# Three products of rounded operands for the routed experts' down product

## What is computed

```python
h = jnp.einsum('nd,edh->enh', xf, We1) + be1[:, None, :]
act = _geglu(h)                       # a * gelu(g), 2*768 -> 768
yE = jnp.einsum('enh,ehd->end', act, We2) + be2[:, None, :]
yr = jnp.einsum('end,ne->nd', yE, w)  # two of 12 experts for each token
return (ys + yr).reshape(B, T, Dm)    # ys: a shared expert, 512 wide
```

## Time and profile before

| | |
|---|---|
| median of 3 runs | 1599.58 us (1596.09 to 1599.82) |
| the profiled execution | 1594.34 us |
| its span, first to last instruction | 1592.6 us |
| mean granted clock of TensorE | 0.975 of full speed |
| PE busy | 1355.6 us (85% of the span) |
| DVE, ACT, POOL busy | 1341.0, 1052.6, 999.5 us |
| first routed tile starts | 1329.31 us into the span |
| start of one steady routed tile to the next | 8.51 us |

### The profile page before, as it was taken

How to read it: one execution, slowest core, us unless ns; L and a number is a source line. 1 busy time by engine, 2 the same in 40 slices (tenths; PEclk the granted TensorE clock), 3 DMA queues, 4 the chain that set the end, 5 groups by cost and what they waited for, 6 DMA issues and landing times. The chain is left out here.

```text
span 1592.6 us, 33551 instructions
## 1 busy us (share of the span) xinstructions
PE 1355.6 (85%) x12668; PEld 1021.4 (64%) x12668; DVE 1341.0 (84%) x1691; ACT 1052.6 (66%) x2450; POOL 999.5 (63%) x832
## 2 busy tenths in 40 slices
PE   5899999999999999878676766776766899999992
PEld 4688888888888888765333333333333688888881
DVE  4799999999999999986599999999999635666662
ACT  4666666666666666535599899899899235555550
POOL 1878888888888888647466666667666341332323
PEclk9999999999999999998899999999999999999996
DMA  4511111111111111006651210200000026888872
GB/s 128 183 43 37 49 37 43 36 50 36 43 43 43 43 36 29 2 1 145 146 114 37 22 25 1 42 5 1 1 2 1 1 71 271 301 307 312 307 259 86
DMA packets 104156, 132.87 MB, mean 83 GB/s; under 512 B 39515, under 2 KB 95266, under 8 KB 100553
## 3 DMA queue, kind: packets, MB, share of 16 engines
q1 hardware_dynamic: 91496, 59.85, 15.1%
q0 software_dynamic: 9312, 67.90, 12.0%
q10 hardware_dynamic: 3200, 3.15, 0.6%
HBM read 110.44 MB, written 14.45 MB: 78 GB/s over the span
## 5 line engine op out<-in xcount | busy, mean ns | idle before, releaser
L555 POOL TENSOR_TENSOR half<-prob 128x512 f32<-128x512 f32 (+1 forms) x208 | 266.9, 1283 | 108.0 <-ACT prob L591 106.5
L587 ACT ACTIVATE prob<-ps_s,mx 128x64 f32<-128x64 f32 (+1 forms) x624 | 152.1, 323 | 235.8 <-DVE prob L700 235.8
L1345 DVE TENSOR_TENSOR state<-ps_u,state 128x1024 f32<-128x1024 f32 x252 | 296.7, 1219 | 4.3
L695 DVE TENSOR_REDUCE mx<-ps_s 128x16 f32<-128x1024 f32 (+1 forms) x208 | 253.1, 1217 | 15.9 <-PE ps_s L628 12.0
L1304 PE MATMUL ps_y<-state,cz 128*32 128x256 f32 x2048 | 247.0, 383 | 2.1 <-DVE state L1345 1.1
L628 PE MATMUL ps_s<-qbd,kT 64*128 64x256 f32 (+1 forms) x1664 | 216.8, 395 | 23.3 <-ACT prob L587 17.7
L1231 ACT ACTIVATE ps_a<-A,dt 128x256 f32<-128x256 f32 x504 | 210.4, 463 | 39.5 <-DVE state L1340 39.5
L700 DVE TENSOR_TENSOR prob<-ps_s,mx 128x832 f32<-128x832 f32 (+1 forms) x208 | 213.0, 1024 | 7.1
L1215 POOL TENSOR_TENSOR state<-direct,state 128x1024 f32<-128x1024 f32 x64 | 151.7, 2370 | 88.6 <-PE ps_y L1304 88.6
L1286 PE MATMUL ps_u<-x_rows,b_diag 48*128 48x256 bf16 x1024 | 79.0, 274 | 147.6 <-DVE state L1345 134.9
L628 PEld LDWEIGHTS ps_s<-qbd,kT 64*128 64x128 f32 (+1 forms) x1664 | 150.5, 184 | 67.6 <-issue 35.1
(11 more groups left out here) (257 smaller groups left out, 3116.7 us busy)
## 6 DMA issues: line engine op xcount, KB each, us to landing
raw<-in_ctxT_dram SPq DMA_DIRECT2D x80, 268.0 KB, 2.8
x_rows<-ssm_x SPq DMA_DIRECT2D x96, 64.0 KB
raw<-in_ctxT_dram SPq DMA_DIRECT2D x16, 261.0 KB, 2.8
b_diag<-zeros SPq DMA_DIRECT2D x2, 2048.0 KB, 9.0
x_slots<-zeros SPq DMA_DIRECT2D x1, 3456.0 KB, 14.1
xg<-x_slots SPq DMA_DIRECT2D x27, 128.0 KB, 5.9
y_slots<-y SPq DMA_DIRECT2D x27, 128.0 KB, 4.8
ssm_x<-xp ACTq DMA_DIRECT2D x8, 384.0 KB, 4.8
```

The costliest lines, as they stand in the source:

```text
L555: pool.tensor_tensor(half[0:rows, :, :], prob[0:rows, g % SLOTS, :, 0:L // 2], prob[0:rows, g % SLOTS, :, L // 2:L], ALU.add).then_inc(hal ...
L695: nc.vector.tensor_reduce(mx[0:rows, g % 2, :], part, AX_X, ALU.max, negate=True)\
L1345: nc.vector.tensor_tensor(h, flat(ps_u[k % 2][:, :, :]), h, ALU.add).then_inc(state_ready, 1)
```

## The change

The down product of the routed experts is done as the up products are: w2 (whole, 128 x 1536) and the turned hidden tile are split into high and low parts in F32R, and PE sums high x high, low x high, high x low. For it:

- ACT makes w2's high part (`split_down_high`) once a tile, right behind the gelu of half 0. It writes the hidden tile's high part where it wrote the F32 copy.
- POOL makes w2's low part (`split_down`) once a tile. In its program the subtraction for tile i-2 stands between the load of w1 and the load of w2 for tile i; the two last ones follow behind all loads.
- DVE makes the hidden tile's low part (`take_turned_low`) twice a tile: for the tile before's half 1 behind x low, ahead of w1 low; for this tile's half 0 behind the product for half 1.
- PE waits for w2's low part (w2_split) instead of w2's load.
- Room is made: gel and hid lie in a buffer of the state space block, the gathered rows in w1's buffers.
- The 8 semaphores of the gathers become 4, one for two row blocks. Another semaphore, in the output product of the state space block, is merged with its neighbour.

```diff
@@ start of experts(): buffers
-        w2 = [sbuf(f"w2_{b}", [P, HR // P * D]) for b in range(BUFS)]
+        w2 = [sbuf(f"w2_{b}", [P, HR // P, D]) for b in range(BUFS)]
+        w2l = [sbuf(f"w2l_{b}", [P, HR // P, D], F32R) for b in range(BUFS)]
+        w2h = [sbuf(f"w2h_{b}", [P, HR // P, D], F32R) for b in range(BUFS)]
...
+        gel, hid = (f["spare"][:, i * HR:(i + 1) * HR].rearrange("p (a n) -> p a n", a=2) for i in range(2))
+        hidT = sbuf("hidT", [P, 2, HS // 2])
+        hidTh = sbuf("hidTh", [P, 2, HR // 2], F32R)
+        hidTl = sbuf("hidTl", [P, 2, HR // 2], F32R)
+        back = [w1[t // 6][:, 2 * D * (t % 6):2 * D * (t % 6 + 1)].rearrange("p (i d) -> p i d", i=2) for t in range(TT)]
...
@@ POOL
+            def load_weights(i, m, w, used):
+                if i >= BUFS:
+                    pool.wait_ge(used, 2 * (TT + i - BUFS + 1))
+                pool.indirect_dma_start(w, None, d[("we1", "we2")[m]][:, :],
+                                        bass.IndirectOffsetOnAxis(ap=weight_row[:, i:i + 1], axis=0))\
+                    .then_inc(w_loaded[m][i % BUFS], 16)
+
+            def split_down(i):
+                pool.wait_ge(w2_high, i + 1)
+                if i >= BUFS:
+                    pool.wait_ge(down_done, 2 * (TT + i - BUFS + 1))
+                pool.tensor_tensor(w2l[i % BUFS][:, :, :], w2[i % BUFS][:, :, :], w2h[i % BUFS][:, :, :].bitcast(F32), ALU.subtract)\
+                    .then_inc(w2_split, 1)
+
             for i in range(RTILES):
...
+                load_weights(i, 0, w1[i % BUFS][:, :], values_done)
+                if i >= 2:
+                    split_down(i - 2)
+                load_weights(i, 1, w2[i % BUFS][:, :, :].rearrange("p c n -> p (c n)"), down_done)
+            for i in range(RTILES - 2, RTILES):
+                split_down(i)
...
-                        .then_inc(y_back[t], 16)
+                        .then_inc(y_back[t // 2], 16)
@@ PE, down
+                    passes = [(hidTh, w2h[b]), (hidTl, w2h[b]), (hidTh, w2l[b])]
...
-                        pe.wait_ge(w_loaded[1][b], (turn + 1) * 16)
+                        pe.wait_ge(w2_split, T - TT + 1)
...
                 for c in range(chunks):
...
+                    for i, (rows, weights) in enumerate(passes):
+                        ins = nc.tensor.matmul(ps_y[:, 0:D], rows[:, half, c * P:(c + 1) * P],
+                                               weights[:, half * chunks + c, :], start=False,
+                                               stop=(half == 1 and c == chunks - 1 and i == len(passes) - 1))
@@ ACT
+                    nc.scalar.copy(hidTh[:, half, 0:w], ps_h[half][:, 0:w]).then_inc(hidT_high, 1)
+
+            def split_down_high(T, turn, b):
+
+                act.wait_ge(w_loaded[1][b], (turn + 1) * 16)
+                if not known(turn, 1):
+                    act.wait_ge(down_done, 2 * (T - BUFS) + 2)
+                nc.scalar.copy(w2h[b][:, :, :], w2[b][:, :, :]).then_inc(w2_high, 1)
...
                     gelu(kind, T, turn, b, half)
+                    if kind == "routed" and half == 0:
+                        split_down_high(T, turn, b)
@@ DVE
+            def take_turned_low(kind, T, turn, b, half):
+
+                if kind == "shared":
+                    return
+                dve.wait_ge(hidT_high, (T - TT) * 2 + half + 1)
+                dve.wait_ge(down_done, T * 2 + half - 1)
+                nc.vector.tensor_tensor(hidTl[:, half, :], ps_h[half][:, 0:HR // 2], hidTh[:, half, :].bitcast(F32),
+                                        ALU.subtract).then_inc(hidT_ready, 1)
...
                 if after:
                     take_x_low(*after)
+                if not known(T, 1):
+                    take_turned_low(*behind(kind, T, turn, b, 0, 1))
+                if after:
                     split_low(*after, 0)
                 multiply(kind, T, turn, b, 1)
+                take_turned_low(*behind(kind, T, turn, b, 1, 1))
                 if not known(T, 1):
                     take_y(*behind(kind, T, turn, b, 0, 1)[:4])
...
             def tail():
+                take_turned_low("routed", TT + RTILES - 1, RTILES // BUFS - 1, BUFS - 1, 1)
                 take_y("routed", TT + RTILES - 1, RTILES // BUFS - 1, BUFS - 1)
                 for t in range(TT):
-                    dve.wait_ge(y_back[t], 32)
+                    dve.wait_ge(y_back[t // 2], 64)
```

More of the change, by code:

```diff
@@ L1383, in ssm_output @@
         mean_ready, rr_ready = sem("so_mean_ready"), sem("so_rr_ready")
-        own_ready, rr_placed, rr_taken = sem("so_own_ready"), sem("so_rr_placed"), sem("so_rr_taken")
+        own_ready, rr_placed = sem("so_own_ready"), sem("so_rr_placed")
         shift_chain = sem("so_shift_chain")
@@ L1457, in turn_tokens @@
                 if p == 3:
-                    pe.wait_ge(rr_taken, 1)
+                    pe.wait_ge(rr_placed, 2)
                 for e in range(2):
@@ L1503, in _ @@
             dve.wait_ge(rr_placed, 1)
-            nc.vector.tensor_copy(rr_tokens[:, :], ps_t[3][:, 0, 0:TT]).then_inc(rr_taken, 1)
-            dve.wait_ge(rr_taken, 1)
+            nc.vector.tensor_copy(rr_tokens[:, :], ps_t[3][:, 0, 0:TT]).then_inc(rr_placed, 1)
+            dve.wait_ge(rr_placed, 2)
             for p in range(TT // 2):
@@ L1677, in experts @@
         y_stored = [sem(f"e_y_stored{b}") for b in range(BUFS)]
-        y_back = [sem(f"e_y_back{t}") for t in range(TT)]
+        y_back = [sem(f"e_y_back{p}") for p in range(TT // 2)]
         x_turned, xTh_ready, xT_ready = sem("e_x_turned"), sem("e_xTh_ready"), sem("e_xT_ready")
@@ L1682, in experts @@
         hid_done, hid_turned, hidT_ready = sem("e_hid_done"), sem("e_hid_turned"), sem("e_hidT_ready")
+        hidT_high, w2_high, w2_split = sem("e_hidT_high"), sem("e_w2_high"), sem("e_w2_split")
         down_done, y_taken, out_ready = sem("e_down_done"), sem("e_y_taken"), sem("e_out_ready")
@@ L1766, in _ @@
             pool.wait_ge(owner_ready, 1)
-            for i in range(RTILES):
[L1770 to L1775, removed]
+            def load_weights(i, m, w, used):
[10 more added lines that the diff above has]
+                    .then_inc(w2_split, 1)
+            for i in range(RTILES):
+                load_weights(i, 0, w1[i % BUFS][:, :], values_done)
[4 more added lines that the diff above has]
+                split_down(i)
             for b in range(BUFS):
@@ L1780, in _ @@
                     j = 2 * t + i
-                    pool.indirect_dma_start(back[:, t, i, :], None, d["y_slots"][:, :],
+                    pool.indirect_dma_start(back[t][:, i, :], None, d["y_slots"][:, :],
                                             bass.IndirectOffsetOnAxis(ap=slot[:, j:j + 1], axis=0))\
-                        .then_inc(y_back[t], 16)
+                        .then_inc(y_back[t // 2], 16)
         @block.tensor
@@ L1825, in down @@
                 if kind == "shared":
-                    weights, biases = f["ws2"][:, :, :], f["sel_shared"][:, :]
+                    passes, biases = [(hidT, f["ws2"])], f["sel_shared"][:, :]
                 else:
-                    weights = w2[b][:, :].rearrange("p (c n) -> p c n", c=HR // P)
+                    passes = [(hidTh, w2h[b]), (hidTl, w2h[b]), (hidTh, w2l[b])]
                     biases = sel[:, bass.ds(T - TT, 1), :].rearrange("p a s -> p (a s)")
@@ L1837, in down @@
                 for c in range(chunks):
-                    ins = nc.tensor.matmul(ps_y[:, 0:D], hidT[:, half, c * P:(c + 1) * P],
-                                           weights[:, half * chunks + c, :], start=False,
-                                           stop=(half == 1 and c == chunks - 1))
+                    for i, (rows, weights) in enumerate(passes):
+                        ins = nc.tensor.matmul(ps_y[:, 0:D], rows[:, half, c * P:(c + 1) * P],
+                                               weights[:, half * chunks + c, :], start=False,
+                                               stop=(half == 1 and c == chunks - 1 and i == len(passes) - 1))
                 ins.then_inc(down_done, 1)
@@ L1900, in take_turned @@
                     act.wait_ge(down_done, q - 1)
-                nc.scalar.copy(hidT[:, half, 0:w], ps_h[half][:, 0:w]).then_inc(hidT_ready, 1)
+                if kind == "shared":
+                    nc.scalar.copy(hidT[:, half, 0:w], ps_h[half][:, 0:w]).then_inc(hidT_ready, 1)
+                else:
+                    nc.scalar.copy(hidTh[:, half, 0:w], ps_h[half][:, 0:w]).then_inc(hidT_high, 1)
[4 more added lines that the diff above has]
+                nc.scalar.copy(w2h[b][:, :, :], w2[b][:, :, :]).then_inc(w2_high, 1)
             def split_high(T, turn, b, half):
@@ L2058, in tail @@
                             c.wait()
-                        ins = nc.vector.scalar_tensor_tensor(out=sb["x"][:, t, :], in0=back[:, t, i, :],
+                        ins = nc.vector.scalar_tensor_tensor(out=sb["x"][:, t, :], in0=back[t][:, i, :],
```

(1 more changed line is left out.)

4 lines of the change are left out of this document (removed).

## The result

The changed kernel took 1606.01 us in the median of seven runs (1602.46 to 1608.40), the kernel before 1599.82 in seven (1595.95 to 1600.98). The ratio over all runs is 1.0048, with a 95% interval of 1.0036 to 1.0060 (the two medians alone give 1.0039): slower by 0.4 to 0.5%. The profiled execution took 1606.66 us, its span is 1604.9. The predicted 1604.4 lies 1.6 us under the median.

The account below looks back on a forecast made before the run. PE bound the routed tiles at 8.51 us. First tile +1.12, 25 tile starts +3.75, wait for x -0.5, last down products and low part -0.6, end +1.0: +4.8 on 1599.58, giving 1604.4; range 1590 to 1613.

Parts of the forecast that it names:

- PE's part: Routed down product: nine rounded products per half, 1.07 us against 1.30, saving 0.46 a tile; 8.05 if nothing else moved.
- The cycle: Routed tile: gelu, w2 high, w2 low, w1 low, next tile; DVE held by POOL's subtraction, tile 8.66 us.
- The price of POOL's subtraction: w2's low part on POOL, 128x1536: 3.52 us at the rate of a 128x536 subtraction, range 3.08 to 3.85.
- The 1.62: DVE's held low part of w1 ends 1.62 us after POOL's subtraction, at +8.52 in the tile.
- PE's start behind DVE: At a routed tile's start, PE begins about 0.14 us after DVE's low part of w1 ends.
- Rival 3: POOL's second load issue, held by DVE, delays its next subtraction 0.7 us in 12 tiles: +13.5, 1613; chance 0.17.
- The sum: All terms from first routed tile to kernel end: +4.8 us, giving 1604.4 on the median.
- the first tile: First routed tile: 8.66 us long, so the second starts +1.12 us later; nothing saved on its down products.
- The wait for x: PE's 0.88 us wait at 1544.53 falls partly into new idle time: -0.5 us.
- The end: Last down products -0.9, low part before the last product +0.3, four sums instead of two after the last landing +1.0.
- Rival 1: Routed tiles: DVE isn't held by POOL, PE stays the bound at 8.05 us a tile: -11.1, 1588.5; chance 0.15.
- rival 2: Routed tiles: POOL's subtraction takes only 3.08 us, tile 8.21: -6.9, 1592.7; chance 0.08.

Follow-up runs that it names:

- first trace of before: Unchanged kernel before the change, its first profiled execution: 1594.34 us, against a median of 1599.58.
- second trace of before: Kernel before the change, unchanged, traced once more: 1595.39 us, tile 8.51 us.
- experiment 9: Changed kernel with w2's low part made on DVE and a fifth gather semaphore, last two row blocks summed singly: 1608.00 us, ratio 0.9945 to the kernel before.
- experiments 1 to 3: Changed kernel with POOL subtracting 48 of 1536 elements, only filling zeros, or subtracting 1280 of 1536: ratios 0.9941, 0.9932, 0.9971 to the kernel before.
- the six pieces: Changed kernel with POOL's subtraction cut into six instructions of one block each: 1627.34 us, ratio 1.0174 to the kernel before.
- experiment 8: Changed kernel with w2's low part made by DVE behind the copy of y, POOL only issuing loads: 1589.32 us, ratio 0.9936 to the kernel before.
- experiment 2: Changed kernel with POOL filling w2's low part with zeros three times instead of subtracting: 1589.02 us, ratio 0.9932 to the kernel before.

## Why the prediction was right, and where it wasn't

- **PE's part**: the nine products go at steps of 0.12 us (1429.84 to 1430.68 in the timeline of the change: seven steps of 0.12), and the tile without the hold is 8.09, where 8.05 was said.
- **The cycle**: w2 high from +1.81, POOL from +3.37 for 3.51 us, DVE's end 1.61 behind it. The prediction had +1.80, +3.38, 3.52 and 1.62. The price of POOL's subtraction, by the row of the same operation at 536 elements, was right to 0.01 us. The 1.62 doesn't come out of the row that it names: 0.29 us for 256 elements is 1.13 ns each, not "little over 1.04", and would give 1.74. The slope between two unheld records (0.42 for 256, 1.76 for 1536) is 1.05 ns and gives 0.29 + 1.34 = 1.63; the measured 1.61 bears that out.
- **PE's start behind DVE** was put at 0.14 us, from two views of one record of PE (1439.10 and 1438.94, which are 0.16 apart); neither tells how long PE takes behind a signal of DVE's, so no row of before gave this term. At 21 tile starts of the loop it is 0.25 (1431.21 to 1431.46); at the five before and behind it 0.10, and the tiles that run between those are 8.6. This term alone is 0.11 us in each of 21 tiles, 2.3 us.
- **Rival 3** came true in small, beside the forecast. In ten tiles the second load issue starts inside DVE's low part and takes about 2.45 us:

```profile
1379.44 1.75 DVE L2052 TENSOR_TENSOR w1l<-w,w1h 128x1536 fp32r<-128x1536 f32 x1
1379.53 2.47 POOL L1776 DMA_INDIRECT w<-in_we_dram,weight_row  x1 [0.30 <-issue]
1382.02 3.52 POOL L1784 TENSOR_TENSOR w2l<-w,w2h 128x1536 fp32r<-128x1536 f32 x1
```

  POOL begins at +3.52 instead of +3.37, and that tile is 8.9 instead of 8.74. I had priced the delay at 0.7 us (and 12 x 0.7 is 8.4, not 8.7). The 0.30 us that lies between two load issues isn't there between a load issue and a subtraction (1382.00 to 1382.02), and DVE begins its other low part earlier than I had it (+0.93, not +1.27). With its true size, 0.17 us in eight of the 20 tiles, it adds 0.07 to the mean tile. Another 0.02 is from the first tile of each turn of the loop, in which gelu, w2 high and POOL all start about 0.08 later.
- **The sum**: the first tile 8.57 where 8.66 was said. From the second to the last start +6.4 us against the first trace of before, where +3.25 stood (3.75 less 0.5). The wait for x that was to be half saved isn't in the second trace of before, and against that trace the figure is +7.5. The points above take the tile from 8.66 to 8.83, in 20 tiles 3.4 us.
- **The end** was put at +0.4 (1.0 for the merged semaphores, less 0.6). From the last tile's start to the end of the span it is 41.5 us, against 42.0 in both traces of before: -0.5. Up to the last copy of y it is 11.5 against 12.4, so the 0.9 of the down products was saved and the 0.3 for the low part didn't show. Behind that copy it is 29.9 against 29.6, and there the path was wrong. The last four sums do start together, and end at 1601.59; the last store is issued 0.03 behind them and lands 1.70 later, as in the kernel before (1588.13 to 1589.83). But neither ends last. POOL's last gather issue ends at 1597.60 in the changed kernel and at 1585.29 in the kernel before, and in both the span ends 7.3 us later; so it does in all twelve traces, while the time from the last sum to the end goes from 3.2 to 4.5 us. The span hangs on POOL's row of issues, not on the sums, so neither the pairs of semaphores nor the fifth one of experiment 9 could show. What POOL does in these 7.3 us the traces don't tell. The 0.3 us are two gather issues that begin inside the sums and take 1.20 and 1.07 us in place of 0.95.
- **The total** was 1.6 us under the median, and part of that is luck: the tiles were put 3.2 to 4.3 us too low, the first tile 0.1 and the end 0.9 too high.
- **Rival 1** (DVE isn't held) is excluded by experiments 1 to 3, **rival 2** (POOL quicker) by the record of 3.51.

So the mechanism of the tile and its order were right, the tile was put 0.17 us too short, and the path at the end was wrong, which the total hides in part.

## What to carry to other kernels

An engine with time to spare is not free if it reads SBUF beside a DVE instruction with two SBUF operands: the subtraction cost 0.74 us a tile on POOL, which had 31% of its time free (8.83 against 8.09), and 0.02 or nothing on DVE (8.11 in experiment 8, 8.09 in 9), which was the busier of the two, but 1.6 us once at the end. Price such an offload by what the held engine was about to release, and look for the place in the cycle, not the share of busy time. Cutting the long instruction up only helps if the cut-up queue has time for the other engine's turns: here the loads wait in that queue, and the six pieces were the worst version.

## What was not expected

- A fill by POOL of 128x1536 takes 1.39 us, and DVE's subtraction runs through it unchanged (experiment 2); the issue of a load, which takes 0.94 us, can be drawn out to 2.5 us by one DVE subtraction of 1.75. It hangs on hundredths of a microsecond: the ten that begin 0.03 to 0.12 behind DVE (as at 1379.53, 0.09 behind) are held; the four that begin 0.01 to 0.02 behind it (as at 1423.68) aren't, and DVE takes 1.80.
- PE starts 0.25 us after DVE's end in the tiles of the loop and 0.10 in the unrolled ones, with the same instructions. Why was not tried.
- Pieces of a POOL subtraction carry a fixed cost of about 0.14 us each: 3.51 us for one, 3.66 for two, 3.79 for three and 4.22 for six that run in one go.
